# A graph network on one Trainium2 core: layer 1's gather products 512 columns wide, and GpSimd's pause per pair of blocks ended by the seventh of its eight gathers

## The chip, the cores and the metric

The kernel runs on one core of one Trainium2 chip. The metric is the device time of one execution in microseconds (us).

## The reference

A residual stream `x` of 6250 nodes by 256 columns passes four steps, each on its layer norm: a GRU graph layer with 100000 typed edges, a small gated feed-forward layer, a second graph layer over the same edges, and a feed-forward layer with 8 experts of which each node takes two. The change lies in the third step:

```python
def _L1_gnn_ref(x, W, b, edge_index):
    src, tgt = (edge_index[0], edge_index[1])
    xt = jnp.einsum('ni,oi->no', x, W) + b
    out = jax.ops.segment_sum(xt[src], tgt, num_segments=num_nodes)
    deg = jax.ops.segment_sum(jnp.ones_like(tgt, dtype=x.dtype), tgt, num_segments=num_nodes)
    out = out / (deg + 1.0)[:, None]
    return out
```

The targets are sorted, and drawn as 6250 u^2 with u uniform, so low-numbered nodes have most of the edges.

## The kernel before

It runs in five parts: set-up; layer 0 (the GRU graph layer and the first feed-forward layer, interleaved); layer 1 (the second graph layer and the router); the experts; the final weighted sum. The graph parts share one gather scheme.

**Edges.** The 100000 edges are 784 chunks of 128. Four chunks (`U` = 4) make a block, so each layer has `BLOCKS` = 196 blocks. One gather on GpSimd (an indirect DMA) fetches the 128 source rows of one chunk from a table in HBM into the ring `rows`, which holds `M` = 8 blocks. A row of `table2` is the normalised node split in two float16 halves, a high and a low one, of 256 columns each: 512 columns, 1 KB.

**Windows.** The 49 tiles of 128 nodes are 49 windows, from the last tile to the first; their size grows from two or three blocks to some 28. VectorE writes a one-hot matrix per chunk (`onehot`), and TensorE multiplies it with the gathered rows into a PSUM bank (`pe_window`): for each chunk once with the high half and once with the low half, both into the same 256 columns. VectorE empties the bank into `sums4` and multiplies it by `inv_deg`, one over the degree plus one (`evacuate2`).

**Groups.** Windows are taken in groups of four (sizes 1, 4, ..., 4, 2, 2). While group g gathers, group g-1 passes four steps: e0 (sums transposed, copied by ScalarE, multiplied by the layer's weights, added to `x_res` and normalised), e1 (router logits), e2 (choice and rank), e3 (lists for the experts). `run_graph` writes out the order of steps and windows on each engine.

**GpSimd's order.** `pool_chunks` issues the gathers, block by block. Blocks go in pairs, an even and an odd one, eight gathers. Before a block's gathers GpSimd waits until the ring slot is free (`free`, semaphore `used` from TensorE). After the sixth gather of the pair it waits until the four of the even block have landed and hands that block to TensorE (`ready`, semaphore `rows_ready`); after the eighth it waits until the odd block's four have landed, hands it over, and only then goes on to the next pair:

```python
if i % 2 == 1 and s == U // 2:
    ready(i - 1, 1)
...
if i + 1 < BLOCKS:
    free(i + 1)
if i % 2 == 1:
    ready(i, 1 if i < BLOCKS - 1 else 1 + PASS - BLOCKS)
```

`settled` is an increment of a semaphore that nobody waits for. Layer 0 uses the same function with its own table.

## Time and profile before

| | us |
|---|---|
| median of 3 runs | 3721.45 (3719.65 to 3723.12) |
| the profiled execution | 3720.04 |
| its span, first to last instruction | 3718.5 |
| layer 1's gathers, first to last start | 1662.33 to 2907.00 |
| GpSimd busy over the span | 1833.6 |
| TensorE busy over the span | 2435.0 |

All rows below are of this one execution. GpSimd's busy time for a gather ends when its descriptors are written, not when the data has landed. A row of the timeline has its start, its length, what ran, and in brackets the idle time of the engine before it and what ended that.

### The profile page before, as it was taken

Reading aid. Unit: us, or ns where it says so; the run is one execution under the profiler, and the core shown is the slowest. Engines: PE = TensorE matmul, PEld = TensorE weight load, DVE = VectorE, ACT = ScalarE, POOL = GpSimd, SP = SyncE. Lnnn points to the kernel's source line nnn. Section 1 sums busy time; section 2 is a strip of 40 time slices with the busy share of each in tenths; the row PEclk is TensorE's granted clock in tenths of the full one; section 3 lists DMA queues with packets and bytes.
Section 4 is the critical chain, followed back from the end, with each engine's and each line's share of the span. In section 5 each row is a group of like instructions: output and inputs, shape, how many; then the busy total and the mean of one; then the engine's idle time right before and its main releaser. Section 6 shows DMA issues by size and latency. Waiting matters only on the chain. (4 is left out here: it accounts for less than half of the span.)

```text
span 3718.5 us, 54160 instructions
## 1 busy us (share of the span) xinstructions
PE 2435.0 (65%) x13318; PEld 1841.3 (50%) x13319; DVE 1525.3 (41%) x3970; ACT 779.4 (21%) x1414; POOL 1833.6 (49%) x2044
## 2 busy tenths in 40 slices
PE   1278887877877674355666655444432499999992
PEld 1255555555544452134444433332221399999992
DVE  6444444444444432034454433232320344545545
ACT  1222232222221121020000000000000145545441
POOL 0363434444565666616666666666666344444441
PEclk7578887888878776566766666556655699999996
DMA  5221222222233222223333333322332222211215
GB/s 135 90 84 57 64 59 66 65 66 65 79 90 86 86 82 86 85 54 88 87 95 88 88 87 89 89 86 83 88 87 85 66 66 85 65 46 64 64 44 219
DMA packets 157829, 303.02 MB, mean 81 GB/s; under 512 B 47366, under 2 KB 91817, under 8 KB 157753
## 3 DMA queue, kind: packets, MB, share of 16 engines
q0 software_dynamic: 85984, 234.74, 21.9%
q1 hardware_dynamic: 40876, 36.11, 3.2%
q10 hardware_dynamic: 30892, 31.40, 2.5%
q14 instruction: 58, 0.47, 0.0%
q8 instruction: 19, 0.31, 0.0%
HBM read 261.73 MB, written 40.39 MB: 81 GB/s over the span
## 5 line engine op out<-in xcount | busy, mean ns | idle before, releaser
L748 POOL DMA_INDIRECT rows<-table,srcT x1568 | 1532.8, 978 | 1172.8 <-DMA rows<-table,srcT 477.6
L817 PE MATMUL bank<-rows,onehot 128*128 x3904 | 763.4, 352 | 818.8 <-POOLq L736 617.2
L817 PEld LDWEIGHTS bank<-rows,onehot 128*128 x3904 | 448.2, 115 | 1118.6 <-issue 967.8
L778 DVE SCALAR_TENSOR_TENSOR onehot<-iota_row,tbase,dstT 128x512 f16 x488 | 366.7, 752 | 783.2 <-issue 506.7
L1779 PE MATMUL bank<-xe_high,W_high 128*128 128x256 f32 x864 | 252.8, 293 | 30.2 <-DVE xe_low L1857 29.9
L1829 ACT ACTIVATE hid<-bank,b 128x256 f32<-128x256 f32 x432 | 181.2, 471 | 346.5 <-PE bank L1781 345.4
L1780 PE MATMUL bank<-xe_low,W_high 128*128 128x256 f32 x864 | 250.6, 290 | 0.0
L1781 PE MATMUL bank<-xe_high,W_low 128*128 128x256 f32 x864 | 250.3, 290 | 0.0
L1779 PE MATMUL bank<-W_high,hid_high 128*128 128x256 f32 x864 | 248.3, 287 | 0.0
L1865 DVE TENSOR_TENSOR hid_low<-hid,hid_high 128x512 fp32r<-128x512 f32 x216 | 149.6, 692 | 235.3 <-ACT hid_high L1833 235.3
L1781 PE MATMUL bank<-W_high,hid_low 128*128 128x256 f32 x864 | 243.9, 282 | 0.0
L1780 PE MATMUL bank<-W_low,hid_high 128*128 128x256 f32 x864 | 243.8, 282 | 0.0
L1468 ACT ACTIVATE sumsT<-bank 128x512 f32<-128x512 f32 (+2 forms) x28 | 13.7, 541 | 872.6 <-PE bank L1423 854.5
L1779 PEld LDWEIGHTS bank<-xe_high,W_high 128*128 128x128 f32 x864 | 171.9, 199 | 32.6 <-issue 32.6
L1733 POOL DMA_INDIRECT xs<-normal,rows_of x110 | 141.2, 1283 | 65.8 <-POOL rows_of L1729 46.3
L1780 PEld LDWEIGHTS bank<-xe_low,W_high 128*128 128x128 f32 x864 | 171.8, 199 | 0.0
L1781 PEld LDWEIGHTS bank<-xe_high,W_low 128*128 128x128 f32 x864 | 171.5, 198 | 0.0
L1780 PEld LDWEIGHTS bank<-W_low,hid_high 128*128 128x128 f32 x864 | 164.5, 190 | 0.0
L1779 PEld LDWEIGHTS bank<-W_high,hid_high 128*128 128x128 f32 x864 | 164.4, 190 | 0.0
L1781 PEld LDWEIGHTS bank<-W_high,hid_low 128*128 128x128 f32 x864 | 164.3, 190 | 0.0
L1742 POOL DMA_INDIRECT results<-ys,to_old x112 | 110.4, 986 | 70.2 <-POOL to_new L1723 53.1
L1833 ACT ACTIVATE hid_high<-hid 128x512 fp32r<-128x512 f32 x216 | 136.5, 632 | 6.9
(338 smaller groups left out, 3591.2 us busy)
## 6 DMA issues: line engine op xcount, KB each, us to landing
rows<-table,srcT POOLq DMA_INDIRECT x1568
W<-in_L_ffn_W_dram SPq DMA_DIRECT2D x14, 1024.0 KB
y<-results ACTq DMA_DIRECT2D x12, 1024.0 KB, 9.9
x_res<-in_x_dram SPq DMA_DIRECT2D x1, 6144.0 KB, 43.0
out_dram<-x_res SPq DMA_DIRECT2D x12, 512.0 KB
table<-part ACTq DMA_DIRECT2D x11, 512.0 KB
normal<-xn ACTq DMA_DIRECT2D x11, 512.0 KB
table<-part SPq DMA_DIRECT2D x6, 512.0 KB, 2.9
```

The lines of the kernel that those rows point to most:

```text
L748: nc.gpsimd.indirect_dma_start(out=rows[:, k % (M * U), 0:ROW], out_offset=None, in_=q.table, in_offset=bass.IndirectOffsetOnAxis(srcT[:, ...
L778: last = nc.vector.scalar_tensor_tensor(onehot[:, ds(slot, U), :], iota_row[:, :].unsqueeze(1).to_broadcast([P, U, P]), base, dstT[:, ds(k ...
L817: last = nc.tensor.matmul(acc[:, 0:cols], hot, ring_rows[:, ds(row0 + (s * q.pitch + at), cols)], start=False, stop=False, skip_group_chec ...
L1468: last = nc.scalar.activation(sumsT[:, c, 0:w * P], bank[c][:, 0:w * P], ACT.Copy)
L1733: nc.gpsimd.indirect_dma_start(out=xs[:, s, :], out_offset=None, in_=normal, in_offset=bass.IndirectOffsetOnAxis(rows_of[:, s:s + 1], axis ...
L1742: nc.gpsimd.indirect_dma_start(out=results, out_offset=bass.IndirectOffsetOnAxis(to_old[:, s:s + 1], axis=0), in_=ys[:, s, :], in_offset=N ...
L1779: nc.tensor.matmul(acc, w_high, m_high, start=start, stop=False)
L1780: nc.tensor.matmul(acc, w_high, m_low, start=False, stop=False)
L1781: return nc.tensor.matmul(acc, w_low, m_high, start=False, stop=stop)
L1829: nc.scalar.activation(hid[:, hc, :], bank[1 + pair][:, o:o + TT], ACT.Gelu, bias=b1[b][:, hc:hc + 1]).then_inc(X["gelu_done"], 1)
L1833: nc.scalar.activation(hid_high[:, both, :], hid[:, both, :], ACT.Copy).then_inc(X["hid_high"], 1)
L1865: nc.vector.tensor_tensor(hid_low[:, both, :], hid[:, both, :], hid_high[:, both, :].bitcast(F32), ALU.subtract).then_inc(X["hid_ready"], 1)
```

## The change

It touches layer 1 alone. (1) `pool_chunks_but_last` takes the place of `pool_chunks` there. The eighth gather of each pair counts on a semaphore of its own (`last_landed`). At the end of a pair GpSimd waits until the other seven have landed, and issues the first gather of the next pair; behind that one it waits for the eighth and hands the odd block over. (2) `pe_window` does one product of 512 columns per chunk, into 512 columns of the bank, so high and low sums lie side by side; the product with zeros that opens a window is 512 columns wide too. (3) ScalarE copies the high sums to `sums4` (`act_high_out`), and VectorE adds the low ones (`evacuate2`). (4) The multiplication by `inv_deg` moves to step e0, where one instruction per tile (256 columns) takes the place of an addition per two tiles (512 columns).

```diff
--- before.py
+++ after.py
@@ -707,6 +707,7 @@
                 self.table, self.with_types = table, with_types
                 self.pitch = PITCH if with_types else ROW
                 self.landed = [sem(f"{name}_rows_landed{m}") for m in range(LANDED)]
+                self.last_landed = [sem(f"{name}_last_row_landed{m}") for m in range(2)]
                 self.rows_ready = sem(name + "_rows_ready")
                 self.frees = sem(name + "_frees")
                 self.used = sem(name + "_used")
@@ -753,6 +754,45 @@
                     if i % 2 == 1:
                         ready(i, 1 if i < BLOCKS - 1 else 1 + PASS - BLOCKS)
 
+        def pool_chunks_but_last(pool, q):
+
...
+                def landed_but_last(i):
+                    share = 16 * U if i % 2 == 0 else 16 * (U - 1)
+                    pool.wait_ge(q.landed[i % LANDED], p * (BLOCKS // LANDED * share) + (i // LANDED + 1) * share)
+                    settled(pool)
+
+                def ready(i, blocks):
+                    landed_but_last(i)
+                    if i % 2 == 1:
+                        pool.wait_ge(q.last_landed[i // 2 % 2], p * (BLOCKS // LANDED * 16) + (i // LANDED + 1) * 16)
+                    pool.sem_inc(q.rows_ready, blocks)
+
+                def free(i):
+                    pool.wait_ge(q.used, pool.value_load(frees[0:1, i:i + 1], min_val=1, max_val=NT * (PASS + 1) + MH))
+                    settled(pool)
+
+                free(0)
+                for i in range(BLOCKS):
+                    for s in range(U):
+                        if i > 0 and s == (U // 2 if i % 2 == 1 else 1):
+                            ready(i - 1, 1)
+                        k = i * U + s
+                        landing = q.last_landed[i // 2 % 2] if i % 2 == 1 and s == U - 1 else q.landed[i % LANDED]
+                        nc.gpsimd.indirect_dma_start(
+                            out=rows[:, k % (M * U), 0:ROW], out_offset=None, in_=q.table,
+                            in_offset=bass.IndirectOffsetOnAxis(srcT[:, k:k + 1], axis=0)).then_inc(landing, 16)
+                    if i + 1 < BLOCKS:
+                        free(i + 1)
+                    if i % 2 == 1 and i + 1 < BLOCKS:
+                        landed_but_last(i)
+                ready(BLOCKS - 1, 1 + PASS - BLOCKS)
+
         def dve_onehots(dve, q, t, late):
 
             if late:
@@ -800,7 +840,8 @@
             first = window_first(pe, t)
             blocks = pe.value_load(windows[0:1, ds(t + NT, 1)], min_val=1, max_val=PASS + 1)
             ring_rows, hots = (ring_[:, :, :].rearrange("p s d -> p (s d)") for ring_ in (rows, onehot))
-            width = D + RELS if q.with_types else D
+            width = D + RELS if q.with_types else ROW
+            spans = ((0, D), (D, width)) if q.with_types else ((0, ROW),)
             nc.tensor.matmul(acc[:, 0:width], zlhs, zrhs[:, 0:width], start=True, stop=False, skip_group_check=True)
             with pe.Fori(0, blocks) as j:
                 m = pe.snap(first + j)
@@ -813,7 +854,7 @@
                 pe.wait_ge(q.rows_ready, m + 1)
                 for s in range(U):
                     hot = hots[:, ds(hot0 + s * P, P)]
-                    for at, cols in ((0, D), (D, width)):
+                    for at, cols in spans:
                         last = nc.tensor.matmul(acc[:, 0:cols], hot, ring_rows[:, ds(row0 + (s * q.pitch + at), cols)],
                                                 start=False, stop=False, skip_group_check=True)
                 last.then_inc(q.used, 1)
@@ -1413,7 +1454,7 @@
         highhot = sb("highhot", [P, 2 * GW, LCOLS - SUB], F32, layer1)
         q2 = Gather("g2", table2, False)
         names = ("gcn_b_loaded filled_ready sumsT_ps sumsT_sb gcn_ps var std xn_ready xnT_ps xnT_sb logit_ps lg_ready ex_ready chosen_ready rank_ps "
-                 "cols_ready spares_ready xn_out lists_hot listed").split()
+                 "cols_ready spares_ready xn_out lists_hot listed high_out").split()
         R = {n: sem("r_" + n) for n in names}
 
         def pe_e0(pe, g, w):
@@ -1494,8 +1535,11 @@
             chain.link(last)
             for half, lo, k in halves(w):
                 dve.wait_ge(R["gcn_ps"], 2 * g + half + 1)
-                xs = x_cols(first_tile(g) + lo, k)
-                last = nc.vector.tensor_tensor(xs, xs, bank[half][:, 0:k * D], ALU.add)
+                for i in range(lo, lo + k):
+                    t = first_tile(g) + i
+                    last = nc.vector.scalar_tensor_tensor(
+                        x_cols(t, 1), bank[half][:, (i - lo) * D:(i - lo + 1) * D], inv_deg[:, ds(t, 1)], x_cols(t, 1),
+                        ALU.mult, ALU.add)
             chain.link(last)
             ln_stats(dve, chain, R["var"], R["std"], g, w, first_tile(g))
             if not (isinstance(g, int) and g == 0):
@@ -1550,13 +1594,19 @@
 
         def evacuate2(dve, g, i):
             t = first_window(g) + i
-            tile = first_tile(g) + slot_of(g, i)
             acc = BANKS2[i] if not (isinstance(t, int) and t == 0) else BANKS2[GW - 1]
             dve.wait_ge(q2.done, t + 1)
+            dve.wait_ge(R["high_out"], t + 1)
+            nc.vector.tensor_tensor(sums4[:, slot_of(g, i), :], sums4[:, slot_of(g, i), :], acc[:, D:ROW],
+                                    ALU.add).then_inc(q2.evacuated, 1)
+
+        def act_high_out(act, g, i):
+            t = first_window(g) + i
+            acc = BANKS2[i] if not (isinstance(t, int) and t == 0) else BANKS2[GW - 1]
+            act.wait_ge(q2.done, t + 1)
             if not (isinstance(g, int) and g == 0):
-                dve.wait_ge(R["sumsT_ps"], g)
-            nc.vector.tensor_scalar(sums4[:, slot_of(g, i), :], acc[:, 0:D], inv_deg[:, ds(tile, 1)], None,
-                                    ALU.mult).then_inc(q2.evacuated, 1)
+                act.wait_ge(R["sumsT_ps"], g)
+            nc.scalar.activation(sums4[:, slot_of(g, i), :], acc[:, 0:D], ACT.Copy).then_inc(R["high_out"], 1)
 
         with nc.Block() as block:
             @block.gpsimd
@@ -1566,7 +1616,7 @@
                                channel_multiplier=0).then_inc(R["cols_ready"], 1)
                 nc.gpsimd.iota(to_list[:, :], pattern=[[0, LCOLS // SUB], [1, SUB]], base=2 * NPAD + 1,
                                channel_multiplier=SUB).then_inc(R["spares_ready"], 1)
-                pool_chunks(pool, q2)
+                pool_chunks_but_last(pool, q2)
 
             @block.tensor
             def _(pe):
@@ -1581,7 +1631,7 @@
                 load_raw(act, 0)
                 load_small(act, 0, 0)
                 act_split(act, 0, 0)
-                run_graph(lambda g, i: None, [lambda g, w: act_e0(act, g, w), lambda g, w: act_e1(act, g, w),
+                run_graph(lambda g, i: act_high_out(act, g, i), [lambda g, w: act_e0(act, g, w), lambda g, w: act_e1(act, g, w),
                                               nothing, nothing, nothing], act)
                 act.wait_ge(R["xn_out"], 16 * (LAST + 1))
```

**GpSimd, layer 1, one pair of blocks before** (a row for each instruction or run of equal ones; `g2_used` is the ring's free slot, `g2_rows_landed0` to `3` the four blocks' landings; the first row is the first gather of a pair, behind the waits that end the pair before):

```order
L748 DMA rows<-table,srcT 128x512 [waits g2_used,g2_rows_landed3]
L748 DMA rows<-table,srcT 128x512 x3
L739 TENSOR_LOAD frees
L739 ISA x2
L748 DMA rows<-table,srcT 128x512 [waits g2_used]
L748 DMA rows<-table,srcT 128x512
L734 REGISTER_ALU
L748 DMA rows<-table,srcT 128x512 [waits g2_rows_landed0]
L748 DMA rows<-table,srcT 128x512
```

The same place now:

```order
L787 DMA rows<-table,srcT 128x512 [waits g2_used,g2_rows_landed3]
L787 DMA rows<-table,srcT 128x512 [waits g2_rows_landed3,g2_last_row_landed1]
L787 DMA rows<-table,srcT 128x512 x2
L777 TENSOR_LOAD frees
L777 ISA x2
L787 DMA rows<-table,srcT 128x512 [waits g2_used]
L787 DMA rows<-table,srcT 128x512
L767 REGISTER_ALU
L787 DMA rows<-table,srcT 128x512 [waits g2_rows_landed0]
L787 DMA rows<-table,srcT 128x512
```

The wait ahead of the first gather counts three landings of the odd block before it where it counted four; the fourth stands ahead of the second gather.

**VectorE, layer 1, end of a group and step e0** (`sums4` filled from the last window's bank, then `x_res` updated and its statistics taken), before:

```order
L1558 TENSOR_SCALAR sums4<-bank7,inv_deg 128x256 [waits r_sumsT_ps,g2_window_done]
L1492 SCALAR_TENSOR_TENSOR x_res<-gcn_b,filled,x_res 128x256 x4
L1498 TENSOR_TENSOR x_res<-x_res,bank0 128x512 [waits r_gcn_ps,layer1_chain]
L1498 TENSOR_TENSOR x_res<-x_res,bank1 128x512 [waits r_gcn_ps]
L193 BN_STATS stats1<-x_res 128x6 [waits layer1_chain]
```

The same place now:

```order
L1600 TENSOR_TENSOR sums4<-sums4,bank7 128x256 [waits r_high_out,g2_window_done]
L1533 SCALAR_TENSOR_TENSOR x_res<-gcn_b,filled,x_res 128x256 x4
L1540 SCALAR_TENSOR_TENSOR x_res<-bank0,inv_deg,x_res 128x256 [waits r_gcn_ps,layer1_chain]
L1540 SCALAR_TENSOR_TENSOR x_res<-bank0,inv_deg,x_res 128x256
L1540 SCALAR_TENSOR_TENSOR x_res<-bank1,inv_deg,x_res 128x256 [waits r_gcn_ps]
L1540 SCALAR_TENSOR_TENSOR x_res<-bank1,inv_deg,x_res 128x256
L193 BN_STATS stats1<-x_res 128x6 [waits layer1_chain]
```

The bank's way to `sums4` now has ScalarE's copy (`r_high_out`) ahead of VectorE's instruction, and the update of `x_res` is in four narrower pieces where it was two.

## Rows read from the trace of the kernel before

**Rows 1.** The page: gathers of both layers (line, engine, count, busy, mean ns, idle), GpSimd's slices

```profile
POOL 0363434444565666616666666666666344444441
...
L748 POOL DMA_INDIRECT rows<-table,srcT x1568 | 1532.8, 978 | 1172.8 <-DMA rows<-table,srcT 477.6
```

**Rows 2.** Busy time by stretch: PE, PEld, DVE, ACT, POOL, clock, DMA share, GB/s

```profile
1687.45:2100.00 412.55, 266.30 (x1194) 182.84 (x1192) 199.39 (x614) 33.81 (x53) 255.95 (x257) 0.66 0.31 90
...
1687.45:2908.00 1220.55, 629.74 (x2807) 416.78 (x2804) 420.18 (x1209) 64.51 (x101) 750.98 (x768) 0.61 0.30 88
```

**Rows 3.** Groups of GpSimd, 1687 to 2908 us: busy, mean ns, idle before and its releasers

```profile
L748 POOL DMA_INDIRECT rows<-table,srcT x768 | 751.0, 978 | 472.1 <-DMA rows<-table,srcT 250.7 <-issue 217.1 <-PE bank L817 4.3
```

**Rows 4.** Waits, 1687 to 2908 us: total us, times, longest

```profile
PE bank L817 <- POOLq L736: 438.0, 112, 7.8
...
POOL rows L748 <- DMA rows<-table,srcT: 250.7, 102, 3.0
```

**Rows 5.** Timeline, 2885 to 2913 us: the last two pairs' gathers and TensorE's blocks

```profile
2885.92 0.94 POOL L748 DMA_INDIRECT rows<-table,srcT  x1 [2.57 <-DMA rows<-table,srcT]
...
2889.67 0.94 POOL L748 DMA_INDIRECT rows<-table,srcT  x1 [0.30 <-issue]
...
2892.17 0.95 POOL L748 DMA_INDIRECT rows<-table,srcT  x1 [0.30 <-issue]
...
2892.85 1.89 PE L817 MATMUL bank<-rows,onehot 128*128 x8 [5.44 <-POOLq L736]
2893.42 0.95 POOL L748 DMA_INDIRECT rows<-table,srcT  x1 [0.30 <-issue]
2894.67 0.95 POOL L748 DMA_INDIRECT rows<-table,srcT  x1 [0.30 <-issue]
...
2897.86 1.89 PE L817 MATMUL bank<-rows,onehot 128*128 x8 [3.12 <-POOLq L736]
2898.25 0.94 POOL L748 DMA_INDIRECT rows<-table,srcT  x1 [2.63 <-DMA rows<-table,srcT]
...
2907.00 0.95 POOL L748 DMA_INDIRECT rows<-table,srcT  x1 [0.30 <-issue]
...
2910.13 1.89 PE L817 MATMUL bank<-rows,onehot 128*128 x8 [3.09 <-POOLq L736]
```

**Rows 6.** Timeline of GpSimd, 2231 to 2242 us: the sixth and seventh gathers of a pair

```profile
2233.88 0.95 POOL L748 DMA_INDIRECT rows<-table,srcT  x1 [0.30 <-issue]
2236.17 0.94 POOL L748 DMA_INDIRECT rows<-table,srcT  x1 [1.34 <-DMA rows<-table,srcT]
```

**Rows 7.** Timeline of GpSimd, 1842 to 1848 us: the second gather of a pair

```profile
1845.30 0.94 POOL L748 DMA_INDIRECT rows<-table,srcT  x1 [2.13 <-issue]
```

**Rows 8.** Waits, 1687 to 2100 us: total us, times, longest

```profile
PE bank L817 <- POOLq L736: 64.3, 22, 7.8
...
POOL rows L748 <- PE bank L817: 1.2, 4, 0.3
```

**Rows 9.** Groups of VectorE, 1687 to 2908 us: step e0 and the emptied banks

```profile
L1558 DVE TENSOR_SCALAR sums<-bank,inv_deg 128x256 f32<-128x256 f32 x47 | 22.6, 482 | 177.2 <-issue 99.3 <-PE bank L820 77.9
...
L1492 DVE SCALAR_TENSOR_TENSOR x_res<-gcn_b,filled,x_res 128x256 f32 x36 | 15.0, 480 | 1.6 <-issue 1.6
L1498 DVE TENSOR_TENSOR x_res<-x_res,bank 128x512 f32 x18 | 12.4, 688 | 56.6 <-PE bank L1430 43.7 <-issue 12.8
```

**Rows 10.** Timeline, 2890 to 2990 us: from the last window to the router's copy

```profile
2911.81 0.22 PE L820 MATMUL bank<-zeros 128*128 128x16 f16 x1
...
2911.88 3.58 PE L1461 MATMUL bank<-highhot,lowhot 128*128 128x408 f32 x8
...
2915.30 0.60 PE L1423 MATMUL bank<-ident,sums 128*128 128x128 f32 x4
...
2922.78 0.38 ACT L1476 ACTIVATE xnT<-bank 128x256 f32<-128x256 f32 x1 [1.72 <-PE bank L1440]
```

5 lines of the change are left out of this document (added).

## The prediction

> **What bounds the kernel now.** I read the page first, then layer 1's gathers by stretch, its waits, and last the timeline of single pairs. On the page GpSimd's slices stand at six tenths through the whole second gather stage, with no slice above or below, and the gathers' idle time is mostly laid to the landing of gathers [rows 1]. Over the 1220.55 us from 1687.45 to 2908 the other engines have room: TensorE is busy 629.74 us, VectorE 420.18, ScalarE 64.51 [rows 2]. Of GpSimd's own time there, 751.0 us is gathers, 217.1 us the 0.30 us that lie between any two, 250.7 us waits for a landing, and 4.3 us waits for TensorE [rows 3]. TensorE in turn waited 438.0 us for GpSimd's semaphore [rows 4]. So the stage runs at GpSimd's pace and the ring is hardly ever full.
>
> One pair of blocks shows the pace [rows 5]. Eight gathers start 1.25 us apart (0.95 us and 0.30 us), then comes a pause: the eighth ends at 2894.67 + 0.95 = 2895.62, the next pair's first starts at 2898.25, 2.63 us later; the pause before it was 2.57 us. From pair to pair that is 2898.25 - 2885.92 = 12.33 us (the mean over 96 pairs is (2898.25 - 1687.45) / 96 = 12.61 us, as some gathers are longer). The 102 waits for a landing [rows 4] are the 97 pauses between 98 pairs and five in the middle of a pair.
>
> **The pause, cut.** Where does 2.6 us come from? TensorE starts on the odd block at 2897.86, 2.24 us after the eighth gather's end, and GpSimd starts again 0.39 us after TensorE. The even block says the same of a landing with others behind it: the fourth gather ends at 2889.67 + 0.94 = 2890.61, TensorE starts at 2892.85, again 2.24 us later [rows 5]. So a gather lands 2.24 us after its end whether or not later ones are under way, and they land as far apart as they are issued, 1.25 us. The seventh then lands 1.25 us before the eighth, and the new pause is 2.63 - 1.25 = 1.38 us.
>
> The wait for the eighth now stands behind the next pair's first gather. That gather would start at 2897.00 and end at 2897.95, and the second could start at 2898.25. The eighth landed for TensorE at 2897.86, and 0.39 us later is 2898.25 too. The two ways tie, so the second wait costs nothing on average but catches every late landing of the eighth. That GpSimd can handle a wait and a semaphore while a gather runs is seen in the same rows: TensorE got the even block at 2892.85, in the middle of the sixth gather (2892.17 to 2893.12), and the seventh came 0.30 us behind the sixth [rows 5]. I take from the scatter of the pauses (2.57 and 2.63) half of it, 0.03 us for each of 97, 2.9 us; the bounds are 0 and 0.06 us (5.8 us). Behind the waiting instruction stand the odd block's hand-over and seven gathers; the hand-over is no later than before, as it follows the same landing.
>
> Gain: 97 x 1.25 = 121.3 us. Once in some 13 pairs there is a stop of 2.13 us between a first and a second gather, seven in the stage, that waits for nothing in the trace [rows 7]; there are more instructions per pair now, so I allow for one more or one fewer, 1.8 us either way, and none in the sum.
>
> **TensorE.** A block was eight products of 256 columns in 1.89 us [rows 5], 0.236 us each. Four of 512 at twice that are the same 1.89 us, and I take this. The bound above is from the nearest wide product, eight of 408 columns in 3.58 us [rows 10]: 0.448 us each, by columns 0.56 for 512, 2.25 us a block, 0.36 us more. The bound below is half the number at the old 0.236, 0.94 us. In a window's life this is hidden while TensorE waits for GpSimd, and late in the stage it waits most of the time. The tight place is the early stretch, where windows are small and the group steps come often. There, to 2100 us, are 33 pairs, GpSimd wants 33 x 1.25 = 41 us back, and TensorE waits 64.3 us for it [rows 8]. 23 us are left.
>
> **The bank's way out.** ScalarE's copy of 256 columns is 0.38 us [rows 10] and comes ahead of VectorE's instruction, at 0.48 us like the one that it replaces (482 ns) [rows 9]. TensorE feels it only where it needs the last window of a group. Step e0's update is four instructions of 0.48 us for two of 0.69: 1.92 - 1.38 = 0.54 us [rows 9]. About one us a group, seven or eight groups in the early stretch, so 8 of the 23 us. With the 0.36 us bound on 66 blocks (24 us) some 9 us would stick out: 3612. At the end of the stage nothing covers step e0. The last window closes at 2911.81, but TensorE turns to its sums at 2915.30 behind eight list products [rows 10], which hide a copy and an addition of 0.86 us. The update is 2 x 0.48 - 0.69 = 0.27 us longer, and that is on the path. Everything behind it, the experts above all, only moves earlier.
>
> **Sum.** 3720.04 (the profiled execution, 1.5 us above its span and 1.4 under the median of the three) - 121.3 + 2.9 + 0.3 = 3601.9; with the 1.4 us to the median, 3603.
>
> **Rivals.**
> *TensorE bounds the early stretch.* If its own chain of windows and steps can't be pressed there, the 33 pairs give nothing and 64 x 1.25 = 80 us are left: 3641. For it: TensorE was busy 266.30 of 412.55 us there [rows 2]. Against it: 64.3 us of waiting, and GpSimd waited for a free slot only 1.2 us [rows 8], with a ring of eight blocks between them.
>
> *The eighth lands later because the next pair has begun.* Once a first gather's packets travel beside it, each 0.1 us of delay is given back, and at 1.25 us all of it: 3721. For it: a wait in the middle of a pair, where landings usually cost nothing, ran to 1.34 us for 0.30 [rows 6], 1.04 us late; a landing can slip so far. Against it: that is five times in a stage, and the fourth's 2.24 us with two more behind it equals the eighth's with none [rows 5]; the DMA engines are busy 0.30 of the time [rows 2] and would be at 0.33.
> The Trainium skill speaks for this rival ("DMA: Bandwidth & Descriptors", section "Latency and other measured facts"): memory answers in 0.2 us on average and in 2 us under high load, and that is most of a transfer's fixed time. By that rule up to 1.8 us could come back per pair, which is more than 1.25; the trace agrees only where a wait ran late [rows 6].
>
> *Slower: the second wait is a second full pause.* If GpSimd, once it has started again, must come to rest for the eighth's landing and needs a fresh 2.6 us behind its first gather, a pair is 12.33 - 1.25 + (2.6 - 0.3) = 13.4 us, 97 x 1.05 = 102 us more: 3823. It decides from 1.25 us at the second gather on. For it: every wait that ended a pair cost 2.57 to 2.63. Against it: the sixth gather, behind which a wait stands, was followed after 0.30 us [rows 5].
>
> **How the numbers follow.** 0.77 for the sum, with 3595 to 3613 as its own range; 0.11 for the early stretch (3641), 0.07 for the late landing (3721), 0.05 for the second pause (3823). The forecast is the likeliest, 3603. The range takes its own range a little beyond, and the early stretch: 3593 to 3642. About 0.2% (7 us) is what a measurement of this kernel can tell from no change; so faster 0.88, same 0.07, slower 0.05.
>
> **What would show it.** GpSimd's idle time before a pair's first gather near 1.4 us and before the second near 0.30; 11.1 us from pair to pair late in the stage; the gathers' idle time for landings down from 250.7 to about 130 us; layer 1's gathers over in some 1124 us; an unchanged layer 0. If the idle time before the second gather is well above 0.30 at most pairs, the step on the tie is wrong. If GpSimd's waits for TensorE are tens of us before 2100, the step on TensorE is wrong. If the pause stays at 2.6, landings don't come one by one.

## The result, and the profile after

| | before | changed |
|---|---|---|
| median of 5 runs, us | 3721.45 (3703.30 to 3729.23) | 3685.05 (3678.28 to 3686.89) |
| ratio, 95% interval | | 0.9897 (0.9874 to 0.9919) |
| profiled execution, span, us | 3718.5 | 3676.7 |
| layer 1's gathers, first to last start, us | 1662.33 to 2907.00, 1244.7 | 1665.18 to 2865.14, 1200.0 |

It is faster, by 36 us and not by 118. Of the 76 us that the profiled execution lacks, layer 1's gathers have nearly all: they take 1200.0 us where 1244.7 - 118 = 1127 was forecast. The page of the changed kernel answers to [rows 1] (`L749` is layer 0's gather now, `L787` layer 1's):

```profile
POOL 0263434444556666526655666666666344444441
...
L749 POOL DMA_INDIRECT rows<-table,srcT x784 | 763.2, 973 | 693.2 <-PE bank L858 256.1
L787 POOL DMA_INDIRECT rows<-table,srcT x784 | 771.0, 983 | 437.4 <-issue 304.0
```

GpSimd's slices are no longer an even six in the second stage: two of them, from 1838 to 2022 us, are fives. (The two further left is the passage between the layers, a one before.) Its timeline late in the stage answers to [rows 5]:

```profile
2797.49 0.95 POOL L787 DMA_INDIRECT rows<-table,srcT  x1 [0.30 <-issue]
2799.76 0.94 POOL L787 DMA_INDIRECT rows<-table,srcT  x1 [1.33 <-DMA rows<-table,srcT]
2801.06 0.94 POOL L787 DMA_INDIRECT rows<-table,srcT  x1 [0.35 <-issue]
...
2810.82 0.94 POOL L787 DMA_INDIRECT rows<-table,srcT  x1 [1.32 <-issue]
2812.08 0.94 POOL L787 DMA_INDIRECT rows<-table,srcT  x1 [0.31 <-issue]
...
2821.88 0.94 POOL L787 DMA_INDIRECT rows<-table,srcT  x1 [1.33 <-DMA rows<-table,srcT]
```

The pause is 1.33 us, the second gather follows after 0.31 to 0.35, and a pair takes 11.06 us (2821.88 - 2810.82). The forecast had 1.38, 0.30 and 11.1. What is not shows in the waits of layer 1 (1690 to 2866 us: total us, times, longest), which answer to [rows 4, 8]:

```profile
DVE onehot L818 <- issue: 390.7, 111, 18.1
...
POOL rows L787 <- PE bank L858: 71.6, 24, 10.9
...
POOL rows L787 <- DMA rows<-table,srcT: 43.3, 35, 2.7
```

and in TensorE's group of products there (busy, mean ns, idle before and its releasers):

```profile
L858 PE MATMUL bank<-rows,onehot 128*128 x956 | 357.3, 513 | 332.6 <-issue 238.2 <-DVE onehot L818 52.6 <-POOLq L774 32.4
```

GpSimd now waits 71.6 us for free ring slots (4.3 before, [rows 3]), 39.6 of them before 2100 us (1.2 before, [rows 8]). TensorE waits 32.4 us for GpSimd's semaphore where it was 438.0 [rows 4]; 238.2 us of its waiting is "issue", time for which the profile knows no releaser. By place in the pair, layer 1's idle time of GpSimd says the same: before the fifth gather, where a wait for a free slot stands, 29.9 us became 87.6, and before the first, where the other one stands, 252.3 became 149.5 and not 131 (252.3 - 121.3). One place shows what that is. The timeline of the changed kernel at 2551 to 2584 us:

```profile
2551.62 0.75 DVE L818 SCALAR_TENSOR_TENSOR onehot<-iota_row,tbase,dstT 128x512 f16 x1 [4.86 <-issue]
...
2553.07 0.59 PE L858 MATMUL bank<-rows,onehot 128*128 x1 [5.14 <-DVE onehot L818]
...
2554.53 0.61 PE L858 MATMUL bank<-rows,onehot 128*128 x1 [0.87 <-issue]
...
2555.86 1.30 PE L858 MATMUL bank<-rows,onehot 128*128 x2 [0.72 <-issue]
...
2559.44 2.11 PE L858 MATMUL bank<-rows,onehot 128*128 x4 [2.29 <-issue]
...
2571.18 1.97 PE L1464 MATMUL bank<-ident,sums 128*128 128x128 f32 x8 [8.63 <-DVE sums L1600]
...
2583.61 0.94 POOL L787 DMA_INDIRECT rows<-table,srcT  x1 [10.88 <-PE bank L858]
```

The four products of one block, back to back elsewhere, stand 0.72 and 0.87 us apart. TensorE falls behind, then has the step e0 of a group to do (from 2571.18), and GpSimd, whose last free slot is used up, stands still for 10.88 us. Between the products the trace has the register instructions of the two engines (start us, length ns, kind, line), which the page leaves out:

```
TensorE                               VectorE
2555.095 697 FUSED_REGOPS 858         2557.258 692 ALU_OP 834
2555.797 707 FUSED_REGOPS 858         2557.982 694 FUSED_REGOPS 834
2557.247 702 ALU_OP 846               2560.103 700 ALU_OP 834
2559.409 707 FUSED_REGOPS 858         2560.836 707 FUSED_REGOPS 834
2560.835 697 FUSED_REGOPS 858
```

They compute ring positions and loop counts. Most take 0.1 us or less (median 74 ns on TensorE, 56 on VectorE); these take 0.70. I counted those of 0.4 to 1.2 us that hold no semaphore wait, while layer 1 gathers: before, 40 of TensorE's 3027 and 37 of VectorE's 1915; changed, 230 of 2044 and 221 of 1933. In the kernel before they come only 4 to 12 us after the last full landing (the end of an idle time of GpSimd of over 2.15 us), and vanish in the pause. By time since the last full landing (TensorE, VectorE and GpSimd together, such instructions per us):

```
since full landing, us     0-4   4-6   6-8   8-10  10-12  12-20    20-38    over 38
before                     0     .01   .08   .22   .10    0        -        -
changed                    .06   .08   .15   .17   .31    .34-.54  .37-.56  .55
```

(From 12 us on the ranges are over steps of 2 us; the longest stretch is 14.4 us before, and 98 us in the changed kernel.) The kernel before has a full landing at the end of every pair and no slow instruction within 4 us of it. The cut pause never waits for everything, and there they go on. That the landing is what ends them is a theory at this point, and the experiments below test a part of it.

### The profile page after: what moved, and what is told of

Read it like the earlier page. It is cut to its first block and busy times, and to the rows that moved or that the text cites. A ratio compares the mean times of both kernels' runs of the same rounds, so it can differ in the third digit from the quotient of the medians.

```text
span 3676.7 us, 51772 instructions
## 1 busy us (share of the span) xinstructions
PE 2404.0 (65%) x12342; PEld 1699.4 (46%) x12343; DVE 1525.9 (42%) x3994; ACT 797.4 (22%) x1463; POOL 1835.8 (50%) x2044
## 5 line engine op out<-in xcount | busy, mean ns | idle before, releaser
L858 PE MATMUL bank<-rows,onehot 128*128 x2928 | 734.1, 393 | 619.4 <-issue 344.4
L749 POOL DMA_INDIRECT rows<-table,srcT x784 | 763.2, 973 | 693.2 <-PE bank L858 256.1
L787 POOL DMA_INDIRECT rows<-table,srcT x784 | 771.0, 983 | 437.4 <-issue 304.0
L858 PEld LDWEIGHTS bank<-rows,onehot 128*128 x2928 | 323.6, 111 | 1014.9 <-issue 892.3
L1829 PE MATMUL bank<-xe_high,W_high 128*128 128x256 f32 x864 | 252.0, 292 | 30.2 <-DVE xe_low L1907 29.9
L1609 ACT ACTIVATE sums<-bank 128x256 f32<-128x256 f32 x49 | 18.7, 382 | 880.1 <-PE bank L861 372.3
```

Of the source, the lines that this page charges most:

```text
L749: nc.gpsimd.indirect_dma_start(out=rows[:, k % (M * U), 0:ROW], out_offset=None, in_=q.table, in_offset=bass.IndirectOffsetOnAxis(srcT[:, ...
L787: nc.gpsimd.indirect_dma_start(out=rows[:, k % (M * U), 0:ROW], out_offset=None, in_=q.table, in_offset=bass.IndirectOffsetOnAxis(srcT[:, ...
L858: last = nc.tensor.matmul(acc[:, 0:cols], hot, ring_rows[:, ds(row0 + (s * q.pitch + at), cols)], start=False, stop=False, skip_group_chec ...
L1829: nc.tensor.matmul(acc, w_high, m_high, start=start, stop=False)
```

## The experiments

Counts and stages of all kernels are of their profiles. "Slow" is TensorE's and VectorE's register instructions of 0.4 to 1.2 us in layer 1; layer 0 and 1 are first to last gather start in us; the last column is GpSimd's waiting for TensorE within layer 1, us (where no instruction is slow, it is all in waits of at most 0.3 us). The five sets ran on five different chips, and the ratio is always to the kernel before on the same chip.

| set, its kernel before | kernel | median us | ratio, 95% interval | layer 0 | layer 1 | slow | waits |
|---|---|---|---|---|---|---|---|
| first result, 3721.45 | before | 3721.45 | | 1448.7 | 1244.7 | 40, 37 | 4.3 |
| | changed | 3685.05 | 0.9897 (0.9874 to 0.9919) | 1452.5 | 1200.0 | 230, 221 | 71.6 |
| one, 3721.4 | pause only | 3688.85 | 0.9926 (0.9905 to 0.9947) | 1451.7 | 1200.9 | 285, 128 | 63.0 |
| | products only | 3720.03 | 0.9998 (0.9986 to 1.0011) | 1444.9 | 1243.9 | 5, 35 | 4.9 |
| | all landed every 2nd pair | 3670.4 | 0.9878 (0.9861 to 0.9894) | 1451.1 | 1190.9 | 45, 119 | 9.5 |
| | no pause | 3732.05 | 1.0044 (1.0027 to 1.0060) | 1452.7 | 1247.9 | 237, 246 | 187.6 |
| two, 3622.23 | all landed every 3rd pair | 3545.9 | 0.9781 (0.9757 to 0.9804) | 1361.4 | 1163.8 | 0, 0 | 10.1 |
| | every 2nd, both layers | 3532.24 | 0.9744 (0.9723 to 0.9765) | 1328.2 | 1181.6 | 0, 0 | 13.1 |
| | rest, all landed | 3647.09 | 1.0058 (1.0040 to 1.0076) | 1360.5 | 1262.2 | 0, 0 | 20.4 |
| | rest, in flight | 3698.53 | 1.0203 (1.0183 to 1.0223) | 1361.6 | 1313.4 | 0, 0 | 5.2 |
| three, 3724.2 | before again | 3720.68 | 0.9993 (0.9980 to 1.0006) | 1448.0 | 1244.1 | 49, 45 | 4.6 |
| | changed again | 3685.04 | 0.9889 (0.9842 to 0.9937) | 1449.0 | 1214.0 | 219, 187 | 82.3 |
| | every 2nd pair again | 3676.92 | 0.9848 (0.9808 to 0.9887) | 1461.5 | 1193.6 | 47, 123 | 17.4 |
| | every 3rd, both layers | 3727.9 | 1.0009 (0.9995 to 1.0022) | 1503.8 | 1191.5 | 82, 124 | 29.5 |
| four, 3619.0 | changed, third time | 3508.04 | 0.9690 (0.9666 to 0.9715) | 1352.9 | 1129.4 | 0, 0 | 6.1 |
| | rest, all landed | 3650.72 | 1.0076 (1.0048 to 1.0104) | 1360.2 | 1262.5 | 0, 0 | 20.1 |
| | rest, in flight | 3697.63 | 1.0208 (1.0182 to 1.0235) | 1361.9 | 1312.0 | 0, 0 | 5.2 |
| five, 3625.62 | rest, all landed | 3649.9 | 1.0078 (1.0057 to 1.0098) | 1362.8 | 1263.1 | 0, 0 | 19.8 |
| | rest, in flight | 3698.32 | 1.0210 (1.0190 to 1.0230) | 1361.6 | 1311.9 | 0, 0 | 4.0 |
| | cut pause in both layers | 3453.99 | 0.9531 (0.9511 to 0.9550) | 1300.5 | 1128.1 | 0, 0 | 7.3 |

**Set one: which half of the change, and does a full landing help?** The theory is that TensorE falls behind because the gathers never all land ("drain"); its rival, that the wide products or the way out of the bank cost it ("products").

*Pause only*: the kernel before, with `pool_chunks_but_last` called for layer 1; products and `evacuate2` as before.

> The cut pause alone, on the kernel before; products, bank and update stay as before. Drain theory (TensorE's and VectorE's register instructions go slow, some 0.7 us each, in stretches that only end when all gathers have landed, and the cut pause no longer lets them all land): the slow instructions come here too, 300 or more in layer 1 against 76 before, TensorE falls behind, GpSimd waits tens of us for free slots, and as a block has twice as many register instructions between its products as in the changed kernel, the time is 3680 to 3715. Product theory (the 512-column product or the longer way out of the bank makes TensorE fall behind): few slow instructions, GpSimd does not wait, 3600 to 3615.

*Products only*: the changed kernel with the old order of waits.

```diff
-                pool_chunks_but_last(pool, q2)
+                pool_chunks(pool, q2)
```

> The wide products, the copy on ScalarE and the four-piece update alone; GpSimd waits for all eight gathers as before. Drain theory: under 100 slow instructions in layer 1, GpSimd hardly waits for TensorE, 3715 to 3725. Product theory: TensorE falls behind here too, GpSimd's waits for TensorE are tens of us, 3730 to 3780.

*All landed every second pair*:

```diff
                     if i % 2 == 1 and i + 1 < BLOCKS:
                         landed_but_last(i)
+                    if i % 4 == 3 and i + 1 < BLOCKS:
+                        pool.wait_ge(q.last_landed[i // 2 % 2], p * (BLOCKS // LANDED * 16) + (i // LANDED + 1) * 16)
+                        settled(pool)
```

> The changed kernel, but at the end of every second pair GpSimd waits for the eighth gather too, so that all gathers have landed once in sixteen. Costs GpSimd 48 x 1.25 = 60 us by itself. Drain theory: the slow instructions fall to well under half of the changed kernel's and stand late in the two pairs; what GpSimd loses in pauses comes back in shorter waits for TensorE: 3655 to 3690. Product theory: GpSimd is slower and nothing comes back beyond the slack: 3695 to 3745.

*No pause*: each hand-over stands in the middle of the next block, so GpSimd never rests.

```diff
-                        if i > 0 and s == (U // 2 if i % 2 == 1 else 1):
+                        if i > 0 and s == U // 2:
...
-                    if i % 2 == 1 and i + 1 < BLOCKS:
-                        landed_but_last(i)
```

> The changed kernel with no pause at all: each block is handed over after the third gather of the next, and GpSimd goes on without waiting at a pair's end, so the gathers come every 1.25 us. GpSimd's own saving would be 97 x 1.35 = 131 us more. Drain theory: the stretches of slow instructions grow to most of layer 1, and nearly all of that saving turns into waits for TensorE: 3650 to 3720. Product theory: TensorE was close to GpSimd's pace anyway and bounds the stage: GpSimd waits for TensorE all along, but the slow instructions stay as few as they are: 3600 to 3680.

The products alone move nothing (0.9998); the pause alone gives the change's gather stage (1200.9 for 1200.0) and its waits for TensorE (63.0 for 71.6). So the products are cleared. A full landing at every second pair costs 48 pauses 1.25 us each, 60 us, and the stage is still shorter than without it, 1190.9 us. The waits of that kernel, 1690 to 2860 us, have TensorE waiting for GpSimd again and the ring free:

```profile
PE bank L861 <- POOLq L774: 235.8, 58, 6.8
PE bank L861 <- issue: 153.2, 68, 5.7
POOL rows L787 <- DMA rows<-table,srcT: 110.1, 53, 3.6
...
POOL rows L787 <- PE bank L861: 9.5, 24, 2.5
```

Without any pause the same list has the opposite. The 100 us that GpSimd does not rest (97 times 1.33 - 0.30) come back as waits for TensorE, 187.6 us for 71.6, and the stage is longer still:

```profile
PE bank L856 <- issue: 261.4, 131, 8.5
POOL rows L787 <- PE bank L856: 187.6, 40, 17.0
```

GpSimd's own register instructions turn slow too in that kernel, 44 of 537 (9 in the changed one). At 3732.05 us it is slower than the 3650 to 3720 expected, and the slow instructions of TensorE and VectorE, 237 and 246, are hardly more than the changed kernel's, so their number doesn't explain the further 48 us of stage. This kernel also hands the odd blocks over one gather later, and nothing here parts the two.

**Set two: how often, and is it the landing or the rest?** *All landed every third pair* has `i % 6 == 5` for `i % 4 == 3`. *Every second pair, both layers* calls the function for layer 0 too:

```diff
-                pool_chunks(pool, q1)
+                pool_chunks_but_last(pool, q1)
```

The two kernels with a rest have an instruction of 1.3 us on GpSimd that does nothing useful, once per pair: ahead of the pair's first gather, so that all land under it, or behind that gather, so that something is always in flight.

```diff
+nc.gpsimd.iota(rest[:, :], pattern=[[1, 1400]], base=0, channel_multiplier=0).then_inc(q.rested, 1)
+pool.wait_ge(q.rested, p * (BLOCKS // 2 - 1) + i // 2 + 1)
```

> The changed kernel, with a wait for the eighth gather too at the end of every third pair, so GpSimd's gathers all land once in three pairs instead of once in two. Drain theory (register instructions of TensorE and VectorE turn slow, about 0.7 us each, some 6 to 11 us after the last time that nothing was in flight, and stay so until nothing is again): two cut pauses of three, by the pace of a pair alone 98 x 11.1 + 33 x 1.25 = 1129 us of gathers, but the slow stretches last from some 8 to 35 us in each run of 36, more than in the run with every second pair (45 of TensorE's register instructions): 100 to 180 slow ones of TensorE, GpSimd waits for TensorE 20 to 50 us, gathers 1185 to 1205 us, kernel 3665 to 3685 us, no better than every second pair. Rival (what matters is only the mean pace asked of TensorE, not how long the gathers run unbroken): the time lies on a line between the drain of every second pair (3670) and none (3685), near 3675, and slow instructions are as many as without a drain, about 230.

> The version with a full wait at every second pair, now in layer 0 too, which had the pause of 2.6 us at every pair. In the kernel before, layer 0's gathers waited 212 us for landings and 256 us for TensorE's ring slots. Drain theory: with the pause short at every second pair only, slow register instructions stay few; the pace of GpSimd rises by 49 x 1.25 = 61 us in what isn't bound by TensorE; about half the stage is, so 15 to 40 us: 3632 to 3658. Rival (layer 0 is bound by TensorE nearly everywhere, and GpSimd's saving turns into waits for ring slots): 3665 to 3675, with layer 0's waits for TensorE up by about 60 us.

> The changed kernel, with an idle GpSimd instruction (an iota of 128 by 1400 into a buffer that nobody reads; by the 128 by 128 and 128 by 208 of the set-up, 224 and 291 ns, an estimated 1.3 us) between the wait for the seventh gather and the next pair's first: the eighth lands under it, so nothing is in flight at its end, though nothing waits for that. Drain theory (slow register instructions end when nothing is in flight): slow instructions of TensorE under 60 as in the kernel before (40), GpSimd's waits for TensorE under 10 us, pairs of about 12.5 us, layer 1's gathers 1240 to 1270 us, kernel 3720 to 3745. Rest theory: the same, so this run stands beside the one with the rest behind the first gather.

> The same idle instruction, but behind the next pair's first gather: GpSimd rests as long per pair, yet at least one gather is always in flight. Drain theory: slow register instructions of TensorE stay many, 150 or more, and GpSimd waits for TensorE at some places, 20 us or more in all, so layer 1's gathers are 1250 to 1290 us, some 10 to 30 us above the run with the rest ahead of the first gather. Rest theory (what counts is how much GpSimd rests per pair, or how fast gathers come): slow instructions under 60 as in the other, times equal within 5 us.

All that these expectations say of slow instructions went untested, and the times missed, for one reason that I had not thought of. On this chip the kernel before takes 3622 us and not 3721, and no profile has a single slow register instruction, in layer 0 or 1. Layer 0, the same code in three of the four kernels, takes 1361 us and not 1450. So the set says nothing on what ends slow instructions; it says that they come on some chips and not on others (or with something else that differed between the sets, as no two sets shared a chip), and that the kernel before is 100 us longer where they are. In layer 0 they are not the whole difference: TensorE has 56 of them there in the kernel before, an excess of some 36 us (56 x 0.65), but its products and other instructions are busy 1056.0 us at a mean granted clock of 0.77, against 988.2 us at 0.81 in the third-pair kernel with the same code in that layer. Whether slow instructions bring the clock down or the clock differs by itself, no run shows. Every second pair in both layers takes 33 us out of layer 0 (1328.2 for 1361), so layer 0 is not all TensorE's, as the rival had it.

The rests differ by 50 us without any slow instruction, so the "equal within 5 us" was wrong for a plain reason. GpSimd's timeline, rest ahead of the first gather:

```profile
2720.22 0.95 POOL L788 DMA_INDIRECT rows<-table,srcT  x1 [0.30 <-issue]
2721.47 0.95 POOL L788 DMA_INDIRECT rows<-table,srcT  x1 [0.30 <-issue]
2723.10 1.29 POOL L795 IOTA rest<- 128x1400 int32 x1 [0.68 <-DMA rows<-table,srcT]
2725.20 0.95 POOL L788 DMA_INDIRECT rows<-table,srcT  x1 [0.81 <-POOL rest L795]
```

and behind it:

```profile
2701.81 0.95 POOL L788 DMA_INDIRECT rows<-table,srcT  x1 [1.31 <-DMA rows<-table,srcT]
2702.76 1.32 POOL L792 IOTA rest<- 128x1400 int32 x1
2705.08 0.95 POOL L788 DMA_INDIRECT rows<-table,srcT  x1 [1.00 <-POOL rest L792]
```

The wait for the seventh is over 0.68 us after the eighth gather's end at the latest, since the iota starts there, but a gather starts only 1.31 us after it. So 0.6 us or more of the cut pause is a gather's own start and no waiting. With the iota ahead, that start is paid once, behind the iota (0.81); with the iota behind, twice (in the 1.31, and 1.00).

**Set three: is it the chip?**

> The kernel before, once more and with its own profile, since the second set of kernels ran on a chip on which the kernel before took 3622 us instead of 3721 and no profile showed a register instruction of 0.4 to 1.2 us. Instruction theory: the chips differ in those slow register instructions alone. If this profile has none on TensorE and VectorE, layer 0 takes about 1361 us of gathers (1449 in the first profile of before), layer 1's 1235 to 1245, the kernel 3615 to 3630; if it has them, 3710 to 3730. Rival (another difference, such as memory): layer 1's gathers differ by tens of us at the same pause of 2.6 us.

> The changed kernel, once more, on the chip of the run beside it. Instruction theory (the gain that was missing went to slow register instructions of TensorE and VectorE): without slow instructions GpSimd's waits for TensorE in layer 1 are under 15 us, its gathers take 1125 to 1150 us, and the ratio to before is 0.967 to 0.976; with them (chip like the first) 0.988 to 0.991, as before. Rival (the missing gain goes to the unbroken gathers themselves, late landings or longer gathers, on every chip): gathers still near 1200 us without any slow instruction, ratio 0.985 to 0.992.

> The changed kernel with a wait for the eighth gather at every second pair, once more. Instruction theory: on a chip without slow instructions the extra wait buys nothing and costs 48 x 1.25 = 60 us, so it is slower than the changed kernel by 20 to 60 us (layer 1's gathers 1175 to 1190 us, ratio to before 0.980 to 0.988); on a chip with them it is faster than the changed kernel by some 15 us, as in the first set. Rival: it is faster than the changed kernel on both.

> The wait for the eighth at every third pair, in layer 0 too. On a chip without slow instructions the same kernel in layer 1 alone was 3546 us for 3622 of before, and every second pair in both layers 3532. I expect layer 0 to gain what GpSimd waited for landings there, 25 to 50 us, most of it already had at every second pair: ratio to before 0.964 to 0.974 without slow instructions. With them (chip like the first) layer 0 and layer 1 lose part of it again: ratio 0.978 to 0.990. Rival (layer 0 is TensorE's): ratio within 0.003 of the layer 1 version, 0.978 on a clean chip.

This chip has slow instructions, and the first result comes back: before 3720.68, changed 3685.04 (0.9889) with a gather stage of 1214.0 us and 82.3 us of waiting for TensorE. A full landing at every second pair again has a shorter stage (1193.6 us), but the intervals of the two ratios, 0.9848 and 0.9889, overlap; that it is better there is likely and not settled. At every third pair it is no better (1191.5). In layer 0 a cut pause does harm on such a chip: its gathers take 1503.8 us instead of 1448, with 112 slow instructions of TensorE for 72, and the whole gain of layer 1 is gone: 1.0009, where 0.978 to 0.990 was expected for such a chip.

**Set four: the changed kernel on a chip without them.** The changed kernel and the two rests once more:

> The changed kernel, a third time, because both sets with it ran on chips with slow register instructions, and the one chip without them never ran it. Instruction theory: on a chip without them (before near 3622) GpSimd waits for TensorE under 15 us in layer 1, the gathers take 1125 to 1150 us, and the ratio is 0.967 to 0.976, the gain that was forecast; on a chip with them (before near 3722) 0.988 to 0.991 once more. Rival (the unbroken gathers themselves lose the time): 0.985 to 0.992 on either.

> The rest of 1.3 us on GpSimd ahead of a pair's first gather, again, for a chip with slow register instructions. Measured on the chip without them: 12.92 us a pair and 1262 us of gathers. Drain theory: everything has landed once per pair, so TensorE has under 80 slow instructions in layer 1 and GpSimd waits for it under 12 us; gathers 1262 to 1275 us. Rest theory: the same. On a chip without slow instructions nothing new is expected: 1.0058.

> The same rest behind a pair's first gather, again. Measured on the chip without slow instructions: 13.43 us a pair and 1313 us of gathers, so GpSimd rests 0.5 us more per pair than in the other, but something is always in flight. Drain theory: on a chip with slow register instructions TensorE has 130 or more of them in layer 1, two or more times as many as with the rest ahead of the first gather, and gathers take 1315 to 1345 us. Rest theory (it is the share of time in which GpSimd writes descriptors that counts): no more slow ones than in the other, under 80. On a chip without them nothing new is expected: 1.0203.

Here the same program gives 0.9690, 111 us for the 118 forecast. Its page, the waits of layer 1 (1594 to 2696 us), and its timeline at the end of the stage:

```profile
L749 POOL DMA_INDIRECT rows<-table,srcT x784 | 763.0, 973 | 593.7 <-DMA rows<-table,srcT 236.2
L787 POOL DMA_INDIRECT rows<-table,srcT x784 | 771.4, 984 | 366.3 <-issue 231.5
```

```profile
PE bank L858 <- POOLq L774: 413.3, 122, 7.6
DVE onehot L818 <- PE bank L858: 244.1, 59, 8.2
...
POOL rows L787 <- DMA rows<-table,srcT: 125.8, 100, 2.6
DVE onehot L818 <- issue: 89.9, 36, 3.6
```

```profile
2682.32 1.89 PE L858 MATMUL bank<-rows,onehot 128*128 x4 [4.53 <-POOLq L774]
...
2686.42 0.94 POOL L787 DMA_INDIRECT rows<-table,srcT  x1 [1.39 <-DMA rows<-table,srcT]
...
2687.20 1.89 PE L858 MATMUL bank<-rows,onehot 128*128 x4 [3.00 <-POOLq L774]
...
2700.20 0.38 ACT L1609 ACTIVATE sums<-bank 128x256 f32<-128x256 f32 x1 [155.38 <-PE bank L861]
2700.69 0.42 DVE L1600 TENSOR_TENSOR sums<-sums,bank 128x256 f32<-128x256 f32 x1 [43.77 <-ACT sums L1609]
...
2707.80 0.88 DVE L1540 SCALAR_TENSOR_TENSOR x_res<-bank,inv_deg,x_res 128x256 f32<-128x256 f32 x2 [5.89 <-PE bank L1471]
```

Beside the same lists of the first result: the busy time of the gathers is the same (771.4 and 771.0 us), TensorE waits 413.3 us for GpSimd again, and VectorE's "issue" is down from 390.7 to 89.9 us. GpSimd's waits for TensorE are 6.1 us in all, and its idle time before the fifth gather is back at 29.9 us. The rival's 0.985 to 0.992 has fallen. So has one that no expectation names, that TensorE's granted clock makes the difference in layer 1. Busy time by stretch shows it (columns as in [rows 2]), the first result's changed kernel ahead of the same kernel on this chip:

```profile
1690.00:2866.00 1176.00, 607.31 (x1841) 284.09 (x1839) 420.97 (x1232) 82.30 (x148) 753.28 (x767) 0.65 0.31 91
```

```profile
1594.00:2696.00 1102.00, 598.68 (x1837) 288.35 (x1836) 417.71 (x1226) 81.82 (x147) 751.28 (x765) 0.63 0.33 97
```

TensorE's clock is not lower where the time is lost (0.65 for 0.63), and its busy time differs by 9 us.

How much of the 111 us is layer 1's is less sure. The kernel before has no profile on such a chip. By an estimate its layer 1 took some 1232 us there: its span of about 3617.5 us, less the 2385 us that the two rests' profiles have outside layer 1's gathers. That leaves some 103 us for layer 1, and the rest is layer 0, which took 1352.9 us in this profile and 1360.2 and 1361.9 in the rests', with the same code.
The full landing, where nothing is slow, costs about what it waits: set two's kernel with one in three pairs has 1163.8 us for 1129.4, 34 us for 32 times 1.25.

**Set five: the two open points.**

> The rest of 1.3 us on GpSimd ahead of a pair's first gather, a third time, for a chip with slow register instructions (it met none so far). There: everything lands once per pair. Drain theory: under 80 slow instructions of TensorE in layer 1, GpSimd waits for it under 12 us, gathers 1262 to 1275 us. Rest theory: the same. On a chip without slow instructions: 1.0058 to 1.0076 as before.

> The same rest behind a pair's first gather, a third time. Drain theory: on a chip with slow register instructions TensorE has 130 or more of them in layer 1, at least twice as many as with the rest ahead of the first gather, and gathers take 1315 to 1345 us. Rest theory: no more than in the other, under 80, and 1312 us. On a chip without slow instructions: 1.0203 to 1.0208 as before.

> The changed kernel with the cut pause in layer 0 too, nowhere a full drain. On a chip without slow register instructions: layer 0 waits there for landings about 210 us at 97 pairs, and gives some of it back to TensorE's ring slots; every second pair in both layers gave layer 0's gathers 1328 us for 1361, so 1300 to 1325 here, and a ratio of 0.955 to 0.964, the fastest kernel of this study. On a chip with them: layer 0 is a stage bound by TensorE for half its time and loses more than GpSimd saves, as with three pairs (1504 us for 1449): layer 0's gathers 1500 to 1600 us and a ratio of 1.00 to 1.03. Rival (layer 0 behaves as layer 1 does): 0.978 to 0.985 there.

This chip has none either, so landing against rest stays open: both rests repeat set two. The cut pause in both layers is the fastest kernel of the study, 3453.99 us, 0.9531, a little under the 0.955 to 0.964 expected. Its one row for both layers' gathers on the page, and its waits in layer 0 (142 to 1450 us):

```profile
L787 POOL DMA_INDIRECT rows<-table,srcT x1568 | 1535.1, 979 | 905.7 <-issue 448.7
```

```profile
POOL rows L787 <- PE bank L858: 197.1, 38, 18.1
POOL rows L787 <- DMA rows<-table,srcT: 118.5, 90, 2.2
```

Layer 0's waits for landings halve from the 236.2 us of the page above, and its gathers take 1300.5 us for the 1353 to 1363 of the others on such chips. It was not run on a chip with slow instructions; the nearest kernel there, every third pair in both layers, gained nothing.

## Why the prediction was wrong, point by point

**The pause.** Right in what it forecast: 1.38 us, median 1.33; the landings do come one by one, 1.25 us apart, whether or not others follow. But a gather doesn't land 2.24 us after its end; that is when TensorE starts on it. Set four's page has 2.7 us from issue to landing, so 1.8 from a gather's end, and the next pair's first gather starts 0.80 us behind the seventh's recorded landing. The difference of two pauses, which the sum uses, is not touched by it.

**The tie at the second gather.** Right: 0.30 to 0.35 us at most pairs. 8 of 98 were over 0.6 us in the first result, 7 before (the stops of [rows 7]), and the mean is 0.44 for 0.43. The tie cost 0.6 us in all, for 2.9 in the sum.

**The products and the bank's way out.** Right. Four products take 1.89 us as forecast, the copy 0.38, the addition 0.42 (0.48 forecast), the step's two updates 0.88 (0.96); the products-only kernel is at 0.9998.

**The cover over TensorE.** This is the step that failed: "the stage runs at GpSimd's pace and the ring is hardly ever full", and with it "Late in the stage it waits most of the time" and the 23 us left in the early stretch. The cover was measured right, but I took what TensorE needs as fixed, so its growing stood in the sum at nothing. Where register instructions turn slow it grows with the cut itself: 40 of them became 230 on TensorE and 37 became 221 on VectorE, and their excess of 0.65 us each is 190 x 0.65 = 124 us and 184 x 0.65 = 120 us of the two engines' time that the sum did not have (they come side by side, so the two don't add up). GpSimd's waits for free slots went from 4.3 to 71.6 us, which is most of the 73 us by which the stage missed its forecast (1200.0 for 1127). 39.6 of them were before 2100 us, which the prediction had named as the sign that this step is wrong. Where no register instruction is slow, the step holds as it was written: 413.3 us of TensorE's waiting, 6.1 of GpSimd's, a gather stage of 1129.4 us for some 1124 forecast, and 125.8 us of waits for landings for "about 130". The 5 us between 1129.4 and 1124 are the gathers' own length, 771.4 us for 766.1 before, which the sum left at nothing (771.0 in the first result). That the ratio too comes out, 0.9690 for 3603 / 3721.45 = 0.968, is in part luck, if layer 0 gave some 8 of the 111 us.

**A sign that was there.** In the kernel before, TensorE's products waited 68.0 us, 46 times, for "issue" in layer 1 (1687 to 2908 us):

```profile
PE bank L817 <- issue: 68.0, 46, 5.6
```

On the chip without slow instructions that group is 2.5 us in the changed kernel. I had read only the groups with a releaser.

**The rivals.** *TensorE bounds the early stretch* came nearest and is not what happened. It gave the loss to the 33 pairs before 2100; in the first result pairs took 12.55, 12.53, 12.04 and 12.02 us by quarters of the stage, for 12.90, 12.80, 12.71 and 12.56 before, so of the 1.25 us some 0.6 to 1.0 are given back in every quarter, more in the first two. Late landing and a second full pause did not occur; the Trainium skill's rule on memory's latency ("DMA: Bandwidth & Descriptors", section "Latency and other measured facts") changed nothing here, as the pause of 1.33 us in the pairs at 2799 to 2822 us shows.

**Shown and not shown.** Shown: the halves of the change; that the loss goes with slow register instructions, by the same program on chips with and without them; that a full landing every second pair takes most of TensorE's away (45 for 230, 47 for 219) and about half or a third of VectorE's (119 for 221, 123 for 187). Only argued: that it is the landing of everything that ends them, since GpSimd's rest grows with it, and the two kernels that part them met no chip with slow instructions. Open: what makes these instructions slow, and why only on some chips; whether the profiler has a part in it, since every timed run has a recorded span and clock too; and how much of layer 0's 90 us between the two sorts of chip is theirs.

## What to carry to other kernels

Cover on an engine that waits holds only as long as the engine's own instructions keep their length: read also its waits without a releaser, and where these are tens of us, look at its register instructions before trusting the cover. A gain of a few per cent on a stage full of register work should be measured on more than one chip: the same change was worth 1.0 and 1.1% in two measurements on chips of one sort, and 3.1% on one of the other. A wait that seems to be pure loss may be what lets another engine catch up; on a chip with slow instructions try it at every second place before taking it out everywhere; on the others taking it out everywhere was best.

## What the runs showed of the hardware

- The same kernel takes 3721 us on some chips and 3622 on others (3619.0 to 3625.62 on three). With layer 0's code as it was, its gathers take 1445 to 1462 us on the first sort, 1353 to 1363 on the second; the set-up (142 to 143 us) and the part behind layer 1's gathers (809 to 818 us) are the same on both.
- On the first sort, register instructions of TensorE and VectorE take 0.70 us instead of mostly less than 0.1 in stretches, on both engines at the same moments and in steps of some 0.71 us (2557.247 and 2557.258, 2560.835 and 2560.836). It is not the code: the same instructions are short elsewhere in the same loop. Instruction fetches are rare (78 packets in the two instruction queues of the changed kernel's page).
- In the kernel before they came 4 us or more after a full landing; in the changed one they rose to 0.55 per us where there had been none for over 38 us. A few of GpSimd's are slow too there (9 of 537), and more with no pause at all (44 of 537).
- A gather's rows have landed 2.7 us after its issue, 1.8 us after its end (changed kernel, third time), at all four places of the odd block.
- A gather starts 0.6 us or more after the wait ahead of it is over: an iota behind the same wait starts 0.68 us after the eighth gather's end, a gather 1.31.
